# The wo_lo passes of y @ Wo on 64 rows, two chunks side by side on the two halves of PE's rows

## What is computed

```
u = x @ Ws + bs                                # (B, T, 64)
state = decay * state + dt * b_t * u_t         # scan over time, per step
y_t   = c_t * state                            # (B, T, 64)
x1 = x + (y @ Wo + bo)                         # Wo: 64 x 512
h_t = tanh(h_{t-1} @ Wh + x1_t @ Wx + b)       # scan over time, 512 wide
out = x1 + h
```

## Time and profile before

| | before |
|---|---|
| median of 3 runs | 1267.18 us |
| profiled execution, its own time | 1265.97 us |
| its span, first to last instruction | 1264.2 us |
| mean granted TensorE clock | 0.98 of full speed |
| PE busy | 94% of the span |
| DVE, ACT, POOL busy | 52%, 40%, 26% |

### The profile page before, as it was taken

The page is one execution under the profiler, slowest core; times in us unless marked ns, Lnnn a source line. Parts: engine busy times, 40 slices in busy tenths (PEclk is TensorE's granted clock), DMA queues, the critical chain, the costliest instruction groups (busy, mean ns, idle before and its releaser), DMA issues.

```text
span 1264.2 us, 17115 instructions
## 1 busy us (share of the span) xinstructions
PE 1187.3 (94%) x5888; PEld 950.0 (75%) x5888; DVE 657.2 (52%) x1022; ACT 504.6 (40%) x756; POOL 333.4 (26%) x179
## 2 busy tenths in 40 slices
PE   4589899998859999999999999999999999999997
PEld 4567758677427888888888888888888888888886
DVE  2135354443996555555554555555555555455553
ACT  1144352443664434344433344443434443334432
POOL 1000000001433443333443333344333344333330
PEclk9899999998889999999999999999999999999999
DMA  9994968938102223222223222222322222322201
GB/s 215 222 216 109 273 145 212 257 98 223 34 0 67 68 91 105 71 66 66 66 69 104 92 66 66 66 66 94 100 71 66 66 66 73 106 87 66 66 34 67
DMA packets 82485, 129.54 MB, mean 102 GB/s; under 512 B 4960, under 2 KB 40800, under 8 KB 82464
## 3 DMA queue, kind: packets, MB, share of 16 engines
q1 hardware_dynamic: 82464, 129.26, 37.5%
HBM read 95.69 MB, written 33.55 MB: 102 GB/s over the span
## 4 chain that ended last, share of the span: by engine, by line
PE 84%; SPq 5%; DVE 4%; DMA 3%; issue 2%; ACT 0%; POOL 0%; DVEq 0%; POOLq 0%; ACTq 0%
PE bank L725 9%; PE bank L733 9%; PE bank L734 9%; PE bank L719 9%; PE bank L718 9%; PE bank L737 9%; PE bank L677 7%; PE bank L656 5%; PE bank L761 4%; PE bank L669 4%; DMA x_ring<-x_rev 3%; SPq L204 3%; PE bank L708 2%; PE bank L709 2%; PE bank L700 2%
## 5 line engine op out<-in xcount | busy, mean ns | idle before, releaser
L324 POOL TENSOR_TENSOR x_lo<-x_f,x_hi 128x512 fp32r<-128x512 f32 x126 | 160.2, 1307 | 556.0 <-ACT x_hi L442 556.0
L453 ACT ACTIVATE h_f<-z_f 128x512 f32<-128x512 f32 x128 | 80.9, 632 | 346.6 <-DVE z_f L612 346.6
L616 DVE TENSOR_TENSOR hT_lo<-bank,hT_hi 128x512 fp32r<-128x512 f32 x128 | 88.5, 691 | 216.1 <-ACT hT_hi L457 216.1
L733 PE MATMUL bank<-wh_hi,hT_hi 128*128 128x512 f32 x512 | 200.5, 392 | 0.0
L734 PE MATMUL bank<-wh_lo,hT_hi 128*128 128x512 f32 x512 | 200.0, 391 | 0.0
L719 PE MATMUL bank<-wx_lo,x_hi 128*128 128x512 f32 x512 | 199.7, 390 | 0.0
L718 PE MATMUL bank<-wx_hi,x_hi 128*128 128x512 f32 x512 | 199.5, 390 | 0.0
L656 PE MATMUL bank<-t_ring,x_ring 128*128 128x128 f32 x1024 | 134.7, 292 | 44.9 <-DMA x_ring<-x_rev 36.2
L656 PEld LDWEIGHTS bank<-t_ring,x_ring 128*128 128x128 f32 x1024 | 128.7, 202 | 52.1 <-issue 38.5
L612 DVE TENSOR_TENSOR z_f<-bank,b_rows 128x512 f32<-128x512 f32 x128 | 88.5, 691 | 132.4 <-PE bank L737 128.5
L318 POOL TENSOR_TENSOR x_lo<-x_f,x_hi 128x2048 fp32r<-128x2048 f32 x32 | 147.9, 4621 | 21.8 <-PE bank L669 21.8
(11 more groups left out here) (67 smaller groups left out, 1418.0 us busy)
## 6 DMA issues: line engine op xcount, KB each, us to landing
x_ring<-x_rev SPq DMA_DIRECT2D x64, 512.0 KB, 12.5
x_f<-x_dtb SPq DMA_DIRECT2D x32, 1024.0 KB, 8.1
out<-x_f SPq DMA_DIRECT2D x31, 1024.0 KB, 5.3
t_ring<-hankel SPq DMA_DIRECT2D x64, 256.0 KB, 11.7
t_ring<-hankel SPq DMA_DIRECT2D x64, 128.0 KB, 11.1
w_f<-Wx SPq DMA_DIRECT2D x1, 1024.0 KB, 5.4
w_f<-Wh SPq DMA_DIRECT2D x1, 1024.0 KB, 5.0
out<-x_f SPq DMA_DIRECT2D x4, 256.0 KB, 2.3
```

Source lines behind the costliest of these rows:

```text
L324: nc.gpsimd.tensor_tensor(x1_lo[:, c], x1_f[:, par, c], f(x1_hi[:, c]), ALU.subtract)\
L733: nc.tensor.matmul(z, hT_hi[:, k], wh_hi[:, k], start=False, stop=False)
```

## The change

A new tile `y_h2` (64 x 512) on rows 0 to 63 holds a second copy of y_hi. ACT makes it from y_hl (`y_copy_low`), behind the hT_hi copy of step 2 and ahead of `x1_copy`. The passes of wo_lo take y_hi alone: for an even chunk the upper 64 rows of wo_lo and y_hl, for an odd chunk the lower 64 rows of wo_lo and y_h2. The order of the passes becomes wo_hi of chunks c and c+1, then wo_lo of chunks c and c+1, and PE waits for `yh2_ready` ahead of the first wo_lo pass. The term wo_lo*y_lo is no longer computed. The count of passes, 8, stays.

```diff
--- before.py
+++ after.py
@@ -105,6 +105,7 @@
         s_f = sb(ctx, "s_f", [P, G, BATCH])
         y_f = sb(ctx, "y_f", [P, G * BATCH])
         y_hl = sb(ctx, "y_hl", [P, G * BATCH], F32R)
+        y_h2 = sb(ctx, "y_h2", [N, G * BATCH], F32R)
 
 
         soft = [x_f[:, 1, i].rearrange("p t b -> p (t b)") for i in range(SOFT_SLOTS)]
@@ -159,6 +160,7 @@
         s_ready = sem("s_ready")
         y_ready = sem("y_ready")
         yhi_ready = sem("yhi_ready")
+        yh2_ready = sem("yh2_ready")
         ylo_ready = sem("ylo_ready")
         wo_done = sem("wo_done")
         x1_ready = sem("x1_ready")
@@ -436,6 +438,10 @@
                 wait(act, wo_done, KC * g)
                 nc.scalar.copy(y_hl[N:P, :], y_f[N:P, :]).then_inc(yhi_ready, 1)
 
+            def y_copy_low(g):
+                act.wait_ge(yhi_ready, g + 1)
+                nc.scalar.copy(y_h2[:], y_hl[N:P, :]).then_inc(yh2_ready, 1)
+
             def x1_copy(g, par):
                 for c in range(KC):
                     act.wait_ge(x1_ready, KC * g + c + 1)
@@ -443,6 +449,7 @@
 
             tanh_c(0, 0)
             y_copy(0)
+            y_copy_low(0)
             x1_copy(0, 0)
             split_x(1, 1)
 
@@ -461,6 +468,7 @@
                         u_copy(g + 1)
                         tanh_c(g + 1, 1 - par)
                     if s == 2:
+                        y_copy_low(g + 1)
                         x1_copy(g + 1, 1 - par)
                     if s == 1 and not (isinstance(g, int) and g == GROUPS - 2):
                         split_x(g + 2, par)
@@ -704,9 +712,13 @@
 
                 pe.wait_ge(yhi_ready, g + 1)
                 pe.wait_ge(ylo_ready, g + 1)
-                for c in range(KC):
+                for c in range(0, KC, 2):
                     nc.tensor.matmul(XB[c][:], wo_hi[:, bass.ts(c, P)], y_hl[:], start=True, stop=False)
-                    nc.tensor.matmul(XB[c][:], wo_lo[:, bass.ts(c, P)], y_hl[:], start=False, stop=True)\
+                    nc.tensor.matmul(XB[c + 1][:], wo_hi[:, bass.ts(c + 1, P)], y_hl[:], start=True, stop=False)
+                    pe.wait_ge(yh2_ready, g + 1)
+                    nc.tensor.matmul(XB[c][:], wo_lo[N:P, bass.ts(c, P)], y_hl[N:P, :], start=False, stop=True)\
+                      .then_inc(wo_done, 1)
+                    nc.tensor.matmul(XB[c + 1][:], wo_lo[0:N, bass.ts(c + 1, P)], y_h2[:], start=False, stop=True)\
                       .then_inc(wo_done, 1)
 
             def z_first(s, after=None):
```

## The result

The changed kernel takes 1282.8 us, the median of 9 runs (1273.85 to 1287.32); the kernel before, in 9 runs beside them, 1267.18 us (1258.15 to 1278.86). The ratio is 1.0108 with a 95% interval of 1.0064 to 1.0152: slower, by 13.7 us (8.1 to 19.3). The profiled execution took 1285.35 us, with a span of 1283.5 us.

The account below looks back on a forecast made before the run. PE was taken to bound the loop of 27.37 us a group, POOL's chain close behind. Pairs -0.235 and shape changes +0.56 gave +0.325 us a group, times 31 +10.1 us: 1277.3 us, range 1265 to 1291.

Parts of the forecast that it names:

- POOL's slack: POOL's x1_lo chain, needed by z_second of the next group's step 0, can come 0.31 us later per group.
- Two pairs: Four wo_lo passes become two side-by-side pairs on PE, second load 0.11 us behind the first: saves 0.235 us a group.
- Four changes of shape: PE's switches between 128 and 64 rows, 0.14 us each between bounds 0 and 0.275: costs 0.56 us a group.
- rival B: PE empties at each change of shape, 0.275 us each: +0.865 us a group, 1294.0 us; chance 0.17.
- Sum on PE: Pairs and changes of shape together on PE: -0.235 + 0.56 = +0.325 us a group.
- The wait for y_h2: PE's wait for ACT's copy before the first wo_lo: 0.08 us, or nothing when a 0.14 us shape change covers it.
- Chunk 0 later: Chunk 0's wo_lo, x1_sum, x1_copy and POOL come 0.37 us later; POOL's chain would end 0.06 later.
- rival A: Changes of shape are free and POOL's chain takes the whole gain: 1267.2 us, or 1264.6 without the wait; chance 0.30.
- The first product at zero: First product, with no recurrence to hide in: at most 0.3 us could be won, once; taken as 0.
- C: ACT's y_h2 copy is late by up to 0.1 us, POOL's chain +0.10 to +0.20: 1270.3 to 1273.4 us; chance 0.08.
- D: The array halves do not run together: no saving, 0.09 us for the wait, +2.8 us, 1270.0 us; chance 0.06.
- E: Pairs and changes cost nothing, POOL's chain does not bind: -0.235 to -0.455 us a group, 1259.9 to 1253.1; chance 0.05.

Follow-up runs that it names:

- e3: Changed kernel with both wo_lo passes of a pair on the same upper 64 rows, reading y_hl; loop period 28.27 us against 27.77.
- e4: Changed kernel in the order wo_hi, wo_lo, wo_hi, wo_lo: eight changes of shape a group, no pair; period 28.97 us over 27 groups.
- e2: Changed kernel with its order, y_h2 copy and wait, but all passes of 128 rows over y_hl; loop period 27.48 us against 27.37 before.
- e5: Changed kernel with all four wo_hi first, then both pairs: two changes of shape a group; loop period 27.92 us against 27.37 before.
- e9: e6 once more, timed against the kernel before: 1276.27 us against 1268.5, ratio 1.0041; loop period 27.36 us.
- e6: e5 with z_second of the next group's step 0 waiting for x1_lo chunk by chunk; loop period 27.34 us against 27.37 before.

## Why the prediction was right, and where it was not

The side (slower), the time (1277.3, in a range of 1265 to 1291; measured 1282.8) and the mechanism held: PE bounds the loop, the pairs save, the changes of shape cost more than that, and POOL's slack is not used up. That the sum came out so close is in part luck, since two of its terms were wrong in opposite directions. By its steps:

- **Two pairs**: side by side was right, the lag was not. The step took 0.11 us between the loads of a pair, saving 0.235 us a group; they start within 0.01 us of each other (720.15, 720.16), and e3 prices the second pass at 0.50/2 = 0.25 us when it can't run beside the first. The saving is the full 0.455. The 0.11 came from a load behind another on the same rows, and is right for that (e3). The Trainium skill (TensorE: Matmul & The Clock Gate, "The mechanism") states that loads overlap passes in flight on another row group and that such tiles start about 4 ns apart. The trace agrees, with 0.00 to 0.01 us between the two loads and between the two passes of a pair; the prediction named this and should have taken it.
- **Four changes of shape**: the term was undersized, 0.14 us each; measured 0.20 (e4, and 0.43 - 0.2275 in the changed kernel's own loads; by the periods, 0.21 in the changed kernel, (0.40 + 0.455)/4, and 0.225 in e3). The middle between the bounds was chosen for want of a nearer row. The weight load is open, as the upper bound had it, and on top of that it waits, but only 0.09 us past the point where a stream would start the next pass (0.32 - 0.2275), not for the whole recorded end of the pass (0.16). The Trainium skill's rule that changing the mode drains TensorE (TensorEngine Tiling (Array Packing), "Key Properties") agrees in kind: the load waits past the point where a stream would go on, though not to the recorded end of the pass. The full price of rival B, 0.275, was too high.
- **Sum on PE**: +0.325 was forecast; -0.455 + 4 x 0.20 = +0.345 by the measured terms. Two errors, -0.22 and +0.24, nearly cancelled. The timeline has +0.37 to L746, and 0.03 more comes behind it, from the seven passes that run 0.231 us apart. The sum is the 0.40 of the period. Why these passes are further apart stays open.
- **The wait for y_h2**: right in size (0.10 in e2 against 0.08), and covered in the changed kernel, as the step said.
- **Chunk 0 later, POOL's slack of 0.31**: right; e5 shows both. In the changed kernel x1_sum starts 1.16 us after the first wo_hi (720.76 - 719.60) against 0.74, 0.42 later where 0.37 was forecast, but PE is later too, so POOL never binds: rival A would have needed a free change. e2 is the nearest thing to A that was run, and it lands at its 0.1 us.
- **The first product at zero**: wrong, +1.2 us once up to z_recur (6.98 us after the first wo_hi pass against 5.82; the other 0.3 of the 1.5 us belongs to the second product). The step counted what could be won and not what the changes cost. PE runs at a granted clock of 0.50 there, where a change costs 0.30 us (see e9), and x1_sum of chunk 3 starts 4.5 us after the first wo_hi pass instead of 3.8. How much of the 1.2 us that makes is open: the clock also rose later than in the kernel before, and e6 and e9, the same kernel, differ by 0.8 us with that alone.
- **Rivals**: C falls by e2 (y_h2 is 0.41 us behind the first wo_hi pass, where C needed over 0.55), D by e3, and E by e4 and e5. B's drain is there, at 0.20 instead of its 0.275. A needed a change under about 0.09.

## What to carry to other kernels

Splitting PE's rows pays one pass per pair and costs two changes per block, so count changes first: here 0.2275 us per pair of 512 columns against 0.20 us or a little more per change. A block of one pair lost 0.20 us (the changed kernel, 0.40 for two blocks), a block of two pairs broke even (e6, e9); longer blocks were not run. Before regrouping to save changes, measure the slack of what the reordered result feeds: 0.31 us at POOL turned a neutral order into +0.56 us, and waits chunk by chunk took it back at no cost. And when a start of varying length blurs the totals, take the period of the loop from one recurring instruction: two executions of one kernel agreed to 0.013 us in 27, while their totals were 1261.6 and 1278.6 us. Yet a period leaves out what happens once: e9's loop ties with the kernel before, and its time does not.

## What was not expected of the hardware

- The price of a change is the same in both directions, 0.20 us at the 2.4 GHz level (e4: five loads in a row 0.43 us apart; 0.20 to 0.225 by the periods of e4, e3 and the changed kernel), and 0.30 at the 1.2 GHz level (first product).
- A release of the transposes that is about 0.1 us late costs nothing, because their first load stands 0.21 us ahead of its pass and gives up part of that lead (e6).
- In the last three groups of e4 the granted clock averages 0.94 and the group takes 1.6 us more, though the instructions are those of the groups before and PE is recorded as busy throughout. The clock falls to 1.2 GHz right behind the product with its eight changes. No other kernel here shows this in its loop, none has more than four changes a group, and the 27 groups before it in e4 do not show it either; what brings the drop on was not tried.
